# Two unused tensors around the buffers of gathered rows, in a recurrent layer with a mixture of experts

## What is computed

```
x = x + ga * recurrence(layernorm(x) * (1 + ca) + sa)
h = layernorm(x) * (1 + cb) + sb
probs = softmax(h @ gate_w)                    # 8 experts
g, m  = top_k(probs per expert, 512)           # of 2048 tokens, for each sequence and expert
y     = gelu(h[m] @ w1[e]) @ w2[e]             # 256 -> 1024 -> 256
out   = x + gb * bf16(sum over experts of g * y, added into the rows m)
```

## Time and profile before

| | |
|---|---|
| median of three runs | 1111.69 us |
| profiled execution, its time | 1117.13 us |
| profiled execution, its span | 1115.3 us |
| TensorE (matmul) busy | 1050.8 us, 94% |
| TensorE (weight load) busy | 928.6 us, 83% |
| ACT busy | 778.9 us, 70% |
| DVE busy | 727.4 us, 65% |
| POOL busy | 460.9 us, 41% |
| mean granted TensorE clock | 0.968 |

### The profile page before, as it was taken

How to read it: one execution, slowest core, us unless ns; L and a number is a source line. 1 busy time by engine, 2 the same in 40 slices (tenths; PEclk the granted TensorE clock), 3 DMA queues, 4 the chain that set the end, 5 groups by cost and what they waited for, 6 DMA issues and landing times.

```text
span 1115.3 us, 18688 instructions
## 1 busy us (share of the span) xinstructions
PE 1050.8 (94%) x6922; PEld 928.6 (83%) x6922; DVE 727.4 (65%) x1680; ACT 778.9 (70%) x1236; POOL 460.9 (41%) x422
## 2 busy tenths in 40 slices
PE   7899999999749999999999999999999999999965
PEld 6778878888638888998899988899888999889855
DVE  5689979998758888875446645556455454447554
ACT  4667968987257887777677577776777766778731
POOL 1133423331324454455444554544544445535532
PEclk8999989999869999999999999999999999999978
DMA  7057746423357445456233435335354442456870
GB/s 251 13 127 205 234 103 154 114 58 57 78 47 188 116 124 156 122 135 146 44 54 81 120 82 121 71 86 134 70 119 84 93 96 44 92 106 179 256 293 39
DMA packets 96892, 130.85 MB, mean 117 GB/s; under 512 B 17313, under 2 KB 82465, under 8 KB 95777
## 3 DMA queue, kind: packets, MB, share of 16 engines
q1 hardware_dynamic: 62960, 84.11, 24.2%
q0 software_dynamic: 33024, 44.75, 22.8%
q10 hardware_dynamic: 816, 0.79, 0.2%
HBM read 78.96 MB, written 42.27 MB: 109 GB/s over the span
## 4 chain that ended last, share of the span: by engine, by line
PE 62%; DMA 3%; issue 2%; ACT 1%; DVE 1%; POOL 1%; SPq 1%; DVEq 0%; ACTq 0%; POOLq 0%
PE psum L1878 30%; PE psum L1901 29%; PE psum L1854 2%; DMA w_raw<-in_L_ffn_w 1%; PE psum L420 1%; DMA w_raw<-ffn_rows 1%; POOL ffn_rows L1547 0%; DMA ffn_rows<-rows_y,idx_cur 0%; ACT rows_in L1640 0%; ACT hf L1670 0%; SPq L1503 0%; DVE w L1700 0%; DVE xT L1743 0%; POOL rows_in L440 0%; ACT w L1633 0%
## 5 line engine op out<-in xcount | busy, mean ns | idle before, releaser
L1878 PE MATMUL psum<-w,hidT 128*128 128x256 f32 x3072 | 371.4, 282 | 9.3 <-issue 8.8
L1878 PEld LDWEIGHTS psum<-w,hidT 128*128 128x128 f32 x3072 | 363.6, 190 | 10.9 <-issue 10.2
L1901 PE MATMUL psum<-xT,w 128*128 128x512 f32 x1536 | 369.5, 396 | 2.7 <-ACT hf L1670 2.4
L1901 PEld LDWEIGHTS psum<-xT,w 128*128 128x128 f32 x1536 | 284.2, 189 | 62.0 <-ACT hf L1670 2.8
L1756 DVE TENSOR_TENSOR hidT<-hf,hidT 128x512 fp32r<-128x512 f32 x256 | 176.2, 692 | 229.7 <-ACT hidT L1674 222.9
L1547 POOL DMA_INDIRECT ffn_rows<-rows_y,idx_cur x120 | 213.3, 1777 | 222.3 <-issue 163.3
L440 POOL DMA_INDIRECT rows_in<-x_rows,idx_cur x128 | 136.5, 1067 | 175.8 <-DVE idx_cur L413 145.7
L1674 ACT ACTIVATE hidT<-hf 128x512 fp32r<-128x512 f32 x256 | 161.8, 632 | 8.1
L1614 ACT ACTIVATE rows_y<-psum,g_cur 128x256 f32<-128x256 f32 x124 | 51.8, 469 | 163.3 <-PE psum L1878 153.3
L1670 ACT ACTIVATE hf<-psum 128x512 f32<-128x512 f32 x256 | 150.8, 589 | 16.4 <-PE psum L1901 4.7
L1640 ACT ACTIVATE rows_in<-rows_in 128x256 f32<-128x256 f32 x128 | 66.3, 594 | 15.4 <-PEq L611 15.4
(11 more groups left out here) (205 smaller groups left out, 1223.7 us busy)
## 6 DMA issues: line engine op xcount, KB each, us to landing
w_raw<-in_L_ffn_w SPq DMA_DIRECT2D x30, 1024.0 KB, 11.4
x_rows<-x SPq DMA_DIRECT2D x16, 516.0 KB, 3.9
x_buf<-in_L_attn_x SPq DMA_DIRECT2D x16, 512.0 KB, 5.8
ffn_rows<-scratch SPq DMA_DIRECT2D x8, 1024.0 KB, 8.2
x_buf<-bias_bc POOLq DMA_DIRECT2D x16, 512.0 KB, 6.6
scratch<-x_rows SPq DMA_DIRECT2D x12, 512.0 KB, 8.0
out_x<-scratch SPq DMA_DIRECT2D x12, 512.0 KB, 9.1
w_raw<-ffn_rows SPq DMA_DIRECT2D x12, 512.0 KB
```

The costliest lines, as they stand in the source:

```text
L1878: ins = pe.matmul(y_tile(u, t), hidT[qs][:, k, t * P:(t + 1) * P], w2_s[n % 2][qm][:, k, :], start=(x_ == 0), stop=(x_ == len(terms) - 1))
L1901: ins = pe.matmul(H_bank[m % 4], w1_s[n % 2][qs][:, k, m * P:(m + 1) * P], xT[qm][:, k, :], start=(x_ == 0), stop=(x_ == len(terms) - 1))
```

## The change

Two tensors that nothing reads or writes are declared: one of 32 bytes a partition ahead of the two buffers, one of 96 bytes between them. No instruction is added, removed or moved. Offsets move: `rows_in0` by 32 bytes, `rows_in1` by 128, and all that is declared behind them by 128. What is declared ahead of them stays.

```diff
-        rows_in = [sbk(f"rows_in{n}", [P, CT, RW]) for n in range(2)]
+        sbk("apart_lists", [P, 8])
+        rows_in = [sbk("rows_in0", [P, CT, RW])]
+        sbk("apart_rows", [P, 24])
+        rows_in.append(sbk("rows_in1", [P, CT, RW]))
```

## The result

Five runs of the changed kernel have a median of 1118.20 us (1117.62 to 1118.55), five of the kernel before 1111.83 us (1110.91 to 1113.85). The ratio is 1.0048, with a 95% interval of 1.0037 to 1.0058, so slower by 5.3 us (4.1 to 6.4); the two medians differ by 6.4 us. The profiled execution of the changed kernel took 1117.98 us, with a span of 1116.2 us.

A forecast was written before the change was run, and what follows sets the result against it. TensorE was taken to bound the kernel, its own lines filling the chain from 488 to about 1005 us. Slow even turns, 5.5 + 0.4 = 5.9 us, on 1111.7 gave 1117.6 us; range 1105.0 to 1119.5, forecast alone 1115.5 to 1119.5.

The forecast's parts named there:

- part 2: `rows_in0` moves 32 bytes: even units' turns (eight transposes each) lead to the slow rhythm, 0.46 us each, 5.9 us in all.
- part 4: DMAs at new offsets: taken as nothing, with 1 us either way for the range.
- No cover: The whole 5.9 us lies on TensorE's own chain, with nothing to hide it.
- Parts 3 and 4: Weights, `xT`, `hidT` and others move 128 bytes, and DMAs: both taken as nothing; bounds 0.46 us a unit and 1 us.
- The sentence that rested on the Trainium skill: Transfer out of `rows_y`: remainder 64 before, 192 after, so 38 beats instead of 34, an estimated 0.5 us more, once.
- Part 5: Kernel's end follows TensorE; the slow stretch near 1062 us is shifted, not hidden, so the 5.9 us reach the end.
- the remainder of `rows_in1` is the slow one: At the transposes: `rows_in1`'s remainder 32 by 64 gives the slow rhythm, so `rows_in0` becomes slow too; chance 0.45.
- reset: Behind the second layer: list products end the rhythm the transposes set, so the pace behind them is 8.36 us in both.
- A: Rival: the new offset is fast for both buffers, odd units gain, 6.0 us faster, 1105.7 us; chance 0.33.
- B: Rival: one buffer stays slow and one fast, or offset isn't the cause; 1111.7 us, give or take 1; chance 0.22.
- the early alternation: Units 1 to 5 alternate in the same step despite counting products, held against a self-feeding alternation; no size given.
- The rule on lines of 16 bytes: SBUF accesses: all moves are multiples of 16, so by that rule alone no pattern changes and time stays 1111.7 us.

The follow-up runs named there:

- e1_behind: Against the kernel before: one unused tensor of 128 bytes behind the two buffers, which stay; all behind moves by 128 bytes. 1113.22 us, ratio 0.9998.
- e3_both_at_0: Against the kernel before: 32 unused bytes between the buffers, 96 behind; `rows_in1` moves by 32 bytes, all behind by 128. 1118.15 us, ratio 1.0055.
- e10_pitch272: Against e6_like_64: buffer rows take 272 numbers instead of 266, moving only each buffer's second to fourth tile. 1111.31 us, ratio 0.9985 to the kernel before.
- e11_like_32: Against the kernel before: unused bytes, 96 ahead of the buffers, 96 between, 64 behind; both at remainder 32 by 128. 1108.23 us, ratio 0.9958.
- e6_like_64: Against the kernel before: unused bytes, 64 ahead of the buffers, 96 between, 96 behind; both at remainder 0 by 128. 1108.29 us, ratio 0.9962.
- e4_swapped: Against the kernel before: same layout, but even units use the second buffer and odd ones the first. 1112.10 us, ratio 0.9996.
- e7_64_on: Against the kernel before: 64 unused bytes ahead of both buffers, none between, 64 behind; both buffers move by 64 bytes. 1115.97 us, ratio 1.0026.

## Why the prediction was right

**The sum.** Forecast were 5.9 us; measured 5.3 by the ratio (4.1 to 6.4), and 6.4 between the medians. On the chain it can be followed. Where it leaves TensorE near the end, POOL's gather starts at 1005.90 us before:

```profile
1005.90 1.03 POOL rows_in L440
```

and 5.93 us later after:

```profile
1011.83 1.04 POOL rows_in L443
```

The parts are these. The eleven even turns from 8 to 28 cost 11 x 0.46 = 5.06 us, as costed (part 2). The twelfth of the forecast, turn 30, does lead to the slow rhythm now, but it costs nothing: at that time, 1036 to 1047 us, the chain lies on transfers and not on TensorE, such as

```profile
1032.31 6.62 DMA out_x<-res_t
```

Turns 2 and 4 were costed at 0.4. The 48 products behind turn 2 take 0.20 longer, those behind turn 4 nothing, since they stayed fast; from the start of the second half to turn 7 the lag grows by 0.20 in all. And 0.67 us came from ahead of the units: the chain's copy of the first unit's gates starts at 325.86 instead of 325.19 us, which part 4 had priced at nothing with 1 us either way. In the twelve kernels of the experiments the first layer of unit 0 starts between 325.1 and 327.3 us without an order by offsets, so I take the 0.67 for scatter of one execution. Without it the change costs 5.26 us on the chain, close to the 5.3 of the ratio. That the chain of the two profiles gives 5.93, just the forecast, is luck: 0.46 and 0.20 us too much in part 2, and 0.67 of scatter.

**What bounds the kernel** was read rightly up to turn 28, where nothing hid the 0.46 us of a turn. "No cover" was wrong for turn 30.

**Parts 3 and 4**, the move of everything behind, were taken as nothing, and e1_behind shows it: 0.9998. The transfer out of `rows_y`, 4.22 us before, took 4.25 after:

```profile
1027.11 4.25 DMA ffn_rows<-rows_y,idx_cur
```

The sentence that rested on the Trainium skill (page "DMA: Bandwidth & Descriptors", section "How a descriptor splits into AXI transactions") had the remainders the wrong way round, since it left out the 16,512 bytes in front: by the addresses of the built program the rows went from 192 to 64 by 256, and by that rule would need 34 beats instead of 38, an estimated 0.4 us less of the 4.22 (4 beats of 38). Neither sign shows in this transfer.

**Part 5** was half wrong. The shift did reach the end in the medians. But the slow stretch of single products near 1062 us, which was to be shifted with the rest, isn't there after. From 1000 us on, TensorE's waits are for ACT, behind loads of sums, instead of "issue" (total, times, longest):

```profile
ACT acc L1625 <- DMA w_raw<-ffn_rows: 20.9, 6, 4.7
...
PEld psum L1904 <- ACT hf L1673: 7.8, 2, 5.3
```

None of the thirteen other profiles has such a stretch either. So I take it for something of the one execution that was profiled, and not of the kernel; the kernel before was profiled only once. It would explain why that execution was 5.4 us over its median, and why the two profiled spans differ by 0.9 us only (1115.3 and 1116.2) while the medians differ by 6.4. Whoever compares the spans of the two profiles alone would call the change neutral.

**The reason given** was right in its first half and too simple in its second. Right: there are two rhythms, where the turned buffers lie has a hand in which one follows, `rows_in0` loses the fast one by its 32 bytes, each loss costs 0.46 us. Too simple: "the remainder of `rows_in1` is the slow one". The trace of before held a sign against it. This is the second layer behind the first turn of `rows_in1`, unit 1's, up to its first counting product:

```profile
L1878 PE MATMUL psum<-w,hidT x48: 276/276/369, 339.3 to 344.7; 128*128 128x256 f32 x48
```

With 276 ns it is fast. Not borne out either is that the list products "reset" the rhythm: the 36 products behind them do have the fast pace in every profile, but what decides the next unit's rhythm passes through them, or e3_both_at_0 and e10_pitch272 could not come out as they did. That both buffers would be slow was inferred from the pair 64 and 96 of before, in which the partner was part of the cause. The same inference from remainders fails for other places: it would have called e3_both_at_0 fast or mixed and e11_like_32 slow, and both came out the other way. The forecast of two slow buffers was luck in part: it was right where the new place of `rows_in0` and the kept remainder of `rows_in1` happened to hold the slow rhythm; the runs don't show that it had to.

**The rivals.** A (both fast) describes real layouts: in e6_like_64 and e11_like_32 the gain is 0.38% and 0.42%, or 4.2 and 4.7 us of a forecast 6.0, and each unit of the chain shows 10.90 and 2.75. B named the second cause: something is passed on from unit to unit (e10_pitch272), though the prediction held the early alternation against it. Just there e4_swapped begins with fast and slow in the order of before, by the unit's number and not by the buffer. The rule on lines of 16 bytes (the Trainium skill, page "SBUF — State Buffer", section "Door 1: The DMA port swizzle") was cited as a case for no change: all whole buffers move by multiples of 16 here (only e10_pitch272 moves tiles inside them by others, 24 and 72 bytes), and these moves made between -0.4% and +0.6%, so that rule alone doesn't tell what an offset does to TensorE's pace.

**What stays open.** What is carried, and how a turn at a given offset changes it; I haven't found a rule that gives all rows of the table. It isn't shown either that TensorE's own reading of the rows is what feels the offset: ACT normalises the same buffers in place, and the gathers write them, and no kernel moved one without the other. Against these speaks only that the slow pace is even over the second layer (281 ns at least and in the median). Also open is whether the rhythm is the same in each execution: the kernels with one rhythm throughout and alike buffers span 0.5 to 1.7 us in two to six executions, those that alternate 4.3 to 9.4 us in eight to twenty-five (e1_behind 1106.82 to 1116.24 us in ten). A cycle that changes its pattern in some executions would do that, and might account for e7_64_on, but only one execution of each was profiled.

## What to carry to other kernels

When the same instructions run at two paces in turn, look for what alternates with them and for the products' distances, not their busy time: here a difference of 4.3 ns in 113.5 is worth 1% of the kernel between the slowest layout and the fastest. An unused tensor of 32 to 96 bytes is a cheap thing to try, but several places have to be measured: a place that is good beside one partner was bad beside another, and reasoning from one observed pair gave the right sign only for some layouts. Compare medians of several executions, since one profiled execution can carry a stall of its own that is as large as the effect.

## What the runs showed of the hardware

- At a granted clock of 1.00 (480 to 1005 us of before), products of 128x128 by 128x256 follow each other every 113.5 or 117.8 ns (10.90 or 11.31 us for 96), and twelve of those by 128x512 take 2.75 or 2.80 us, with no wait in either case.
- Which of the two holds depends on the offsets of the buffers that are turned (a move of 32 bytes is enough, e1_behind against e3_both_at_0) together with what the units before left. Cycles of one, two and three units were seen with the same instructions.
- One bfloat16 product of 8 columns between turn and second layer made all second layers from unit 6 on slow (11.41 us with the product), but not those before. Behind 16 products of the same kind (L420) the next 36 products took 8.36 or 8.37 us in every unit from 8 on, whatever the rhythm ahead.
- The fastest layouts, 1108.23 and 1108.29 us, beat the kernel before by 0.4% with nothing but unused bytes, and the changed kernel by 0.9%.
